# Rings of four in the expert slot loop, two mixed slots moved, and the mixed slots' weights issued by GpSimd

## The reference, cut to what matters

```
# 16 experts, width I = 352, each token goes to K = 4 of them
cw = combine_weights(x, gate_w)                    # [T, 16], 4 nonzeros per token
for e in range(16):
    a = silu(x @ gate[e].T) * (x @ up[e].T)        # [T, 352]
    out = out + cw[:, e:e+1] * (a @ down[e].T)     # [T, 512]
out = out + swiglu_shared(x) ; return residual + out
```

## Time and profile before

| | |
|---|---|
| median of 3 runs | 1296.19 us (1291.11 to 1301.31) |
| the profiled execution | 1297.71 us, of which 1295.9 us is the span of the trace |
| mean granted TensorE clock | 0.981 of full |
| TensorE busy | 1232.2 us, 95% of the span |
| VectorE / ScalarE / GpSimd busy | 65% / 28% / 26% |
| slot loop, first G to the end of the span | 720.88 to 1295.9 us |

### The profile page before, as it was taken

The page is one execution under the profiler, slowest core; times in us unless marked ns, Lnnn a source line. Parts: engine busy times, 40 slices in busy tenths (PEclk is TensorE's granted clock), DMA queues, the critical chain, the costliest instruction groups (busy, mean ns, idle before and its releaser), DMA issues.

```text
span 1295.9 us, 26339 instructions
## 1 busy us (share of the span) xinstructions
PE 1232.2 (95%) x8747; PEld 747.5 (58%) x8747; DVE 844.3 (65%) x2352; ACT 366.9 (28%) x808; POOL 340.1 (26%) x401
## 2 busy tenths in 40 slices
PE   7979999999998999999999999999999899999995
PEld 6857777877776555444444555554555455554552
DVE  4897688768769475244511577676767676876772
ACT  4754656654453323220000011111111111111111
POOL 1202324322333122114653012121212222121212
PEclk9989999998998999999999999999999999999998
DMA  5443953753663595275446876959596877868562
GB/s 165 83 60 85 146 122 79 155 129 66 129 128 125 131 218 116 89 242 190 174 179 235 254 198 159 221 115 233 125 254 153 227 179 194 197 177 216 124 151 25
DMA packets 205089, 202.41 MB, mean 156 GB/s; under 512 B 71584, under 2 KB 153504, under 8 KB 202912
## 3 DMA queue, kind: packets, MB, share of 16 engines
q1 hardware_dynamic: 120864, 112.25, 32.9%
q10 hardware_dynamic: 67456, 54.24, 16.8%
q0 software_dynamic: 16640, 34.24, 12.6%
HBM read 123.76 MB, written 81.08 MB: 158 GB/s over the span
## 4 chain that ended last, share of the span: by engine, by line
PE 46%; DMA 7%; ACTq 2%; issue 1%; DVE 1%; ACT 0%; POOLq 0%; DVEq 0%
PE pD L2423 10%; PE pG L2410 10%; PE pU L2410 9%; DMA xs<-slot_rows 5%; PE pD L2391 4%; PE pG L2372 4%; PE pU L2372 4%; PE pD L2420 2%; PE pG L2406 2%; PE pU L2406 1%; DMA out<-y,ix_mixed 1%; ACTq L2209 1%; ACTq L2223 1%; PE pU L2366 1%; PE pD L2386 0%
## 5 line engine op out<-in xcount | busy, mean ns | idle before, releaser
L2299 DVE STREAM_TRANSPOSE ups<-a 32x96 f32<-32x96 f32 (+1 forms) x1136 | 296.6, 261 | 35.2
L2183 POOL DMA_INDIRECT out<-y,ix x64 | 99.7, 1558 | 392.9 <-DVE ix L2323 178.5
L2410 PE MATMUL pG<-w,xsT 128*128 x512 | 167.4, 470 | 15.2 <-DVE xsT L2288 13.7
L2423 PE MATMUL pD<-w,ups 128*128 (+1 forms) x384 | 178.2, 599 | 1.9 <-DVE ups L2299 0.7
L2410 PE MATMUL pU<-w,xsT 128*128 x512 | 162.0, 459 | 0.0
L973 PE MATMUL pProj<-front_region 128*128 128x256 f32 x624 | 155.6, 393 | 2.2 <-ACT front_region L708 1.6
L2410 PEld LDWEIGHTS pG<-w,xsT 128*128 128x128 f32 x512 | 96.7, 192 | 94.9 <-issue 54.6
L2239 ACT ACTIVATE g<-pG 128x352 f32<-128x352 f32 x72 | 33.4, 464 | 367.0 <-DVE ix L2323 173.6
L2410 PEld LDWEIGHTS pU<-w,xsT 128*128 128x128 f32 x512 | 97.5, 190 | 54.5 <-issue 0.5
L973 PEld LDWEIGHTS pProj<-front_region 128*128 128x128 f32 x624 | 113.8, 192 | 20.4 <-ACT front_region L708 2.1
L2423 PEld LDWEIGHTS pD<-w,ups 128*128 128x128 f32 (+1 forms) x384 | 70.7, 190 | 85.8 <-issue 78.7
(11 more groups left out here) (312 smaller groups left out, 1787.1 us busy)
## 6 DMA issues: line engine op xcount, KB each, us to landing
w<-in_expert_T SPq DMA_DIRECT2D x16, 1920.0 KB, 8.8
front_region<-in_expert_T ACTq DMA_DIRECT2D x64, 352.0 KB
slot_rows<-zeros SPq DMA_DIRECT2D x72, 266.0 KB, 7.3
xs<-slot_rows ACTq DMA_DIRECT2D x288, 64.0 KB
front_region<-in_expert_T ACTq DMA_DIRECT2D x32, 256.0 KB
front_region<-in_L_attn_hidden_states SPq DMA_DIRECT2D x16, 256.0 KB, 4.2
x2r<-in_L_attn_hidden_states SPq DMA_DIRECT2D x16, 256.0 KB, 4.8
partial_sums<-x2r SPq DMA_DIRECT2D x16, 256.0 KB, 3.2
```

Of the source, the lines that this page charges most:

```text
L2183: pool.indirect_dma_start(out=flat, out_offset=bass.IndirectOffsetOnAxis(ap=to[:, 0:1], axis=0), in_=y[1 - par][:, :], in_offset=None, bou ...
L2299: dve.transpose(aT[par][B * to:B * to + B, 0:n, rows], a[rows, 0:len(IC) * P].rearrange("p (c n) -> p c n", c=len(IC))[:, 0:n, B * to:B * ...
L2410: mm = pe.matmul(out[:, 0:I], rows[:, k, :], w[:, bass.ds(weights[0], 1), 2 * I * k + at:2 * I * k + at + I], start=(k == 0), stop=(k == D ...
L2423: return pe.matmul(out[:, :], gated_[0:m, c, :], w[0:m, bass.ds(weights[0], 1), at:at + D], start=(c == 0), stop=(c == 2))
```

## The change

1. **Rings of four** (`RING = 4`). Four buffers each for the rows (`xs`), metas (`mt`), results (`y`), weights (`wq`) and indices (`ix`). Rows and results take the place of the shared expert's `xg` buffers in `front_region`, so the rows below show them by that name. `load_rows` asks four slots ahead and `load_meta` two. Each wait on a buffer's last user refers to the slot four back instead of two.
2. **Mixed slots** stand at 7, 16, 25, 34, 43, 52, 60 and 68 (`MIXED_AT`), not at 61 and 70. The formula of `until` follows: `lm + (lm + 2) // 8` in place of `lm + lm // 8`.
3. **The mixed slots' weight pieces are issued by GpSimd**, two per slot (`PIECES = 2`), in seven slots from the one behind the last mixed slot on. They stand behind the add of slot q-1. ScalarE issues none.

```diff
-STEP = NQ // NM
-MIXED = STEP - 2
+MIXED_AT = [9 * m + 7 - max(0, m - NM + 3) for m in range(NM)]
-PIECES = 3
+PIECES = 2
+RING, AHEAD = 4, 2
...
-    xs = [sb(f"xs{i}", [P, D]) for i in range(2)]
+    xs = [xg[0][:, i, :] for i in range(RING)]
-    y = [sb(f"y{i}", [P, D]) for i in range(2)]
-    mt = [sb(f"mt{i}", [P, RW - D]) for i in range(2)]
+    y = [xg[1][:, i, :] for i in range(RING)]
+    mt = [sb(f"mt{i}", [P, RW - D]) for i in range(RING)]
...
+            def part_of(q):
+                for m in range(NM):
+                    begin = MIXED_AT[m - 1] + 1 if m else 0
+                    if begin <= q < begin + DC + len(IC):
+                        return m, q - begin
+                return None
...
             def body(q, par):                                  # GpSimd
                 if first(q):
+                    pool.wait_ge(s_routed, 1)
+                    pool.wait_ge(s_gp, 1)
+                    load_mixed(*part_of(q))
                     return
                 pool.wait_ge(s_y, q)
                 pool.wait_ge(s_ex, q)
...                                                             # the add(s) of slot q-1
+                if part_of(q):
+                    load_mixed(*part_of(q))
...
-                least(act, s_xT, q - 1)                        # ScalarE, load_rows
+                least(act, s_xT, q - RING + 1)
...
-                    least(act, s_add, 16 * adds_before(q - 2)) # ScalarE, before y
+                    least(act, s_add, 16 * adds_before(q - RING))
-                if PIECES * (q % STEP) < 2 * (DC + len(IC)) and q < NQ:
-                    load_mixed(q // STEP, q % STEP)
...
-                least(dve, s_y, q - 1)                         # VectorE, take_meta
-                least(dve, s_add, 16 * adds_before(q - 1))
+                least(dve, s_y, q - RING + 1)
+                least(dve, s_add, 16 * adds_before(q - RING + 1))
```

More of the change, by code:

```diff
@@ L1782 @@
 NQ = NF + NM
-STEP = NQ // NM
-MIXED = STEP - 2
+MIXED_AT = [9 * m + 7 - max(0, m - NM + 3) for m in range(NM)]
 NS = 3
-PIECES = 3
+PIECES = 2
+RING, AHEAD = 4, 2
 def is_mixed(q):
-    return q % STEP == MIXED
+    return q in MIXED_AT
 def before_mixed(q):
-    return max(0, (q + STEP - 1 - MIXED) // STEP)
+    return sum(at < q for at in MIXED_AT)
 def adds_before(q):
@@ L1804, in block_of @@
 def block_of(q):
-    return NF + q // STEP if is_mixed(q) else q - before_mixed(q)
+    return NF + before_mixed(q) if is_mixed(q) else q - before_mixed(q)
 assert sorted(block_of(q) for q in range(NQ)) == list(range(NQ))
-assert all(q == i + (i + 1) // 8 for q in range(NQ) if not is_mixed(q) for i in [block_of(q)])
+assert all(q <= i + (i + 3) // 8 <= q + 1 for q in range(NQ) if not is_mixed(q) for i in [block_of(q)])
 def routing(nc, es, counts, scratch, lg, xall, pos, lists, s_pos, s_read, s_routed, route, s_xall):
@@ L2172, in _, with load_mixed @@
             flat = out.rearrange("b t d -> (b t) d")
+            def part_of(q):
[4 more added lines that the diff above has]
+                return None
+            def load_mixed(m, part):
+                for piece in range(PIECES * part, min(PIECES * part + PIECES, 2 * (DC + len(IC)))):
+                    h, c = piece % 2, piece // 2
+                    n, at, width = (P, 2 * I * c, 2 * I) if c < DC else (IC[c - DC], UPW + D * (c - DC), D)
+                    rows = weights_from(pool, "mixed", 2 * m + h)
+                    pool.dma_start(wm[0:n, h, at:at + width], rows[0:n, at:at + width]).then_inc(s_wm, 16)
             def body(q, par):
                 if first(q):
+                    pool.wait_ge(s_routed, 1)
+                    pool.wait_ge(s_gp, 1)
+                    load_mixed(*part_of(q))
                     return
@@ L2203, in _, with load_rows, load_meta, rows_by @@
             mv = xs_d.rearrange("(q p) c -> q p c", p=P)
-            def load_rows(q, par):
-                least(act, s_xT, q - 1)
+            def load_rows(q):
+                least(act, s_xT, q - RING + 1)
                 for b in range(BLOCKS):
[L2209 to L2223, removed]
+                    act.dma_start(xs[q % RING][B * b:B * b + B, :].rearrange("p (a c) -> p a c", a=BLOCKS),
+                                  xv[block_of(q)][:, :, P * b:P * b + P]).then_inc(s_xl[q % RING], 16)
+            def load_meta(q):
+                least(act, s_ex, q - RING + 1)
+                act.dma_start(mt[q % RING][:, :], mv[block_of(q)][:, D:RW]).then_inc(s_ml[q % RING], 16)
+            def rows_by(q):
+                return min(NQ, q + 1 + AHEAD + min(q, RING - AHEAD))
             def body(q, par):
@@ L2228, in body @@
                         act.wait_ge(s_scat[i], 16 * NT * K // 2)
[L2229 to L2235, removed]
+                    load_rows(0)
+                    load_meta(0)
+                    load_rows(1)
+                    load_meta(1)
+                for r in range(max(2, rows_by(q - 1)), rows_by(q)):
+                    load_rows(r)
+                if q + AHEAD < NQ:
+                    load_meta(q + AHEAD)
                 if not end(q):
```

38 lines of the change are left out of this document (19 added, 19 removed).

## The result

The changed kernel takes **1350.49 us** (median, 1347.15 to 1352.21), the kernel before 1293.65. The ratio is **1.0433**, with a 95% interval of 1.0398 to 1.0468. The profiled execution has a span of 1349.1 us against 1295.9, so 53.2 us are to be found.

The account below looks back on a forecast made before the run. TensorE was taken to bound the kernel, with 29.6 us of late starts in its slot loop. 1297.7 - 26 (rings) - 1.2 (end) + 55.6 (new waits) + 8 (clock) = 1334 us; range 1303 to 1368.

Parts of the forecast that it names:

- The new wait: TensorE before the eight mixed slots' G: waits for the last pieces' landing, 55.6 us in sum.
- Slots 7, 60 and 68: Mixed slots with no slot between last pair and G: waits of 11.9, 12 and 10.7 us.
- Slots 16, 25, 34, 43, 52: Mixed slots with one slot between: 4.5 us each beside an expert load, 3 at slot 43.
- The clock: G behind the waits: 1.8 us for each of three long waits, 0.5 for five others, 8 us.
- `until`: Release of expert loads: both formulas keep the counts and the loads their slots; nothing gained or lost.
- The rings: Buffers in the slot loop: four-deep rings remove 26 us of late starts, between 13.7 and 29.6.
- rival 4: GpSimd's chain of adds takes over what the rings free: rings give at worst 13.7 us; in the forecast's spread.
- The pieces leave ScalarE: ScalarE's queue: relief of 112 pieces, some 120 us, counted at nothing beyond the rings' 26 us.
- The end: Last adds after the loop: with 68 as last mixed slot, 1.2 us less.
- 1 and 2, short waits: Mixed slots: low bound, waits 38.3 us, 1305 us, chance 0.16; last pair nearly in time, 23 us, 1290, chance 0.10.
- rival 3: GpSimd's queue: pieces over 2.8 us bound kernel, some 1385 us, chance 0.10; quoted rule: VectorE's two-port copies block descriptor writing.
- high bound of 1377: Whole kernel, forecast's own terms at their highest: waits 78.6 us, clock 14.4, rings only 13.7, giving 1377 us.

Follow-up runs that it names:

- e2: Kernel before with only the pieces' timing changed: two per slot in seven slots, ScalarE issuing, two-deep buffers; 1337.06 us, ratio 1.0346.
- e3: Changed kernel with three pieces per slot instead of two, still issued by GpSimd; 1283.57 us, ratio 0.9927 to the kernel before.
- e11: Changed kernel with the last mixed slots back at 61 and 70, two pieces per slot by GpSimd; 1336.60 us, ratio 1.0358 to before.
- e5: Changed kernel with each expert load let go two finished Ds later; 1336.46 us, ratio 1.0376 to the kernel before.
- e1: Kernel before with the rings of four alone, old places, ScalarE issuing three pieces per slot; 1284.94 us, ratio 0.9926.
- e7: Changed kernel with three pieces per slot by GpSimd and mixed slots at the old places; 1266.73 us, ratio 0.9838 to before.
- e12: Repeat of e3 (changed kernel, three pieces per slot) on another chip, the same as e13's; 1275.57 us, ratio 0.9884 to before.
- e13: Repeat of e7 (changed kernel, three pieces per slot, old places); 1271.88 us, ratio 0.9863 to the kernel before.
- e4: Changed kernel with the same pairs in the same slots issued by ScalarE behind y; 1326.82 us, ratio 1.0236 to the kernel before.
- e8: Changed kernel with three pieces per slot, issued by ScalarE instead of GpSimd, new places; 1286.93 us, ratio 0.9967 to before.
- e6: Kernel before with GpSimd issuing the pieces, three per slot, two-deep buffers, old places; 1289.74 us, ratio 0.9966.

## Why the prediction was right, point by point

- **The new wait** at eight mixed slots, behind D, y, the add, the pair and a landing: right in place and in cause, as the semaphore's times, e2, e3 and e11 show. Forecast 55.6 us, measured 66.5. The sum is nearer than its terms: the three tight slots came out 5.2 us shorter than forecast, the five others 16.1 longer.
- **Slots 7, 60 and 68**: 11.9, 12 and 10.7 forecast, 9.5, 12.1 and 7.8 measured. A piece was mis-sized, which is most of it: I took 1.7 us, and a pair took 1.7 to 1.8 in all. The pair's issue also starts 1.06 us after the add's, before the add's 1.66 are over, so from the add's start it is 2.8 instead of 5.0. The landing was the 3.5 that I took (1298.4 to 1301.9). At slot 60, beside a load, the piece's price doesn't enter: there the add's landing sets the time, as forecast.
- **Slots 16, 25, 34, 43, 52**: 21 us forecast, 37.1 measured, the largest error of the sum. The mechanism was right (e5), but I took the load's landing from the kernel before, 11.9 us behind the end of D. The whole bundle needed 14.4 there (840.46 to 854.8): the add came 2.9 behind D, took 10 us instead of 8.4 to land, and the pair landed 1.3 later. For slot 43 I counted 3, it was 6.9: a load one slot earlier holds up the add before, and so the issue of the last pair. That chain I had left out.
- **The clock**: 8 us forecast, 17.3 measured. I priced a fall at 1.8 for long waits and 0.5 for the others. All eight waits brought the clock down, and G took up to 2.4 longer, with U behind it slow in part.
- **`until`**: right. The third load went out at 841.32, behind D(13), and the last at 1221.9, behind D(58).
- **The rings**: 26 forecast, 28.6 measured in the changed kernel. Alone they give 17.6 (e1), and some 5 to 6 are given back at the end, where the adds' chain is behind, as rival 4 had it. So that 26 came near is in part luck: the other 11 of the 28.6 don't come from the rings alone. They come with either of two things. With GpSimd as issuer and hardly a wait (e7) 2.6 of late starts are left, and in e3, e7, e12 and e13 the last add comes 4.4 to 5.8 us behind D(71). With ScalarE as issuer and the long waits (e4) TensorE waits only 0.5 us for `g`, none for rows, and the last add comes 4.5 us behind D(71): the waits give the other engines time to catch up. The changed kernel has both.
- **The pieces leave ScalarE**, counted at nothing: this step was wrong, and with it the reason that the rings would have hidden a late ScalarE. e8 against e3 and e12 puts it at 5 to 11 us of time once the rings are there, e7 against e1 at 9 us of late starts. In e6 without the rings it is 1% at most. In the changed kernel it stays hidden: e4 shows next to none of it, since the long waits cover it.
- **The end**: 1.2 forecast, 2.1 measured.
- **Rivals.** 1 and 2, short waits: no. 3, GpSimd as the bound: no; an add and its pair are out 2.8 us behind the add's start, of a slot's 7.3. Its adds did grow from 1.56 to 1.66 where a pair follows them, but no wait came of it. That the adds' records kept their length says little about the rule quoted under rival 3: VectorE's time in a slot is mostly stream transposes (4.64 and 0.70 us), not copies, so it was hardly put to the test.
- **The sum** of the deviations: 10.9 more waits, 9.3 more clock, 2.6 and 0.9 less by rings and end, 16.7 above the forecast of 1334; the profiled execution took 1350.7. 1350.5 lies in the range. The high bound of 1377 left out the 1.2 of the end; with it it is 1376, which changes nothing.

## What to carry to other kernels

Where a load is spread over slots of a pipeline, count the engine's own products between the last piece's trigger and its user, not the slots by number: here the body "in front of" the mixed slot was triggered by the product directly ahead of the one that needed it. Two pieces per slot or three was a matter of 5%, more than all else in the change. And take the change apart before dropping it: the rings and GpSimd as issuer, with three pieces per slot and the old places, beat the kernel before by 1.4 to 1.6%, and the rings alone by 0.7%.

## What the runs showed of the hardware

- Two direct DMAs of 96 to 128 rows with their readings of the expert's number took GpSimd 1.7 to 1.8 us, hardly more than one add (1.66), and the first began 1.06 us after the add's start, while its record still ran.
- The adds did not suffer from pieces behind them in GpSimd's queue: the 80 landings sum to 444 us after, 439 in e7 and 444 in e6, against 471 before and 470 in e1, where ScalarE issues the pieces. Over all kernels with one add at a time it is 433 to 450 with GpSimd as issuer and 469 to 480 with ScalarE.
- A piece beside an expert load landed late: the last one of slot 68, with no load near it, landed 3.5 us after it was out; that of slot 16 took 8.6 and in e4 that of slot 60 11.8, and both had gone out within 5 us behind the start of a load.
- After waits of 7 to 12 us the granted clock was 0.56 to 0.72 over the ten microseconds around the next product; after waits of 3 us it sometimes fell (slot 34 in e3, G of 4.28 us) and sometimes didn't (slot 60 there, 2.59).
